# A four-layer cross-attention kernel: layer 2's attention worked in among layer 1's FFN, and layer 3's first queries prepared beside layer 2's gate

## The reference, cut to what matters

```
x = x + tanh(gx[0]) * L0_attn(ctx, ln(x));  x = x + tanh(gf[0]) * L0_ffn(ln(x))
x = x + tanh(gx[1]) * L1_attn(ln(x), ctx);  x = x + tanh(gf[1]) * L1_ffn(ln(x))
x = x + tanh(gx[2]) * L2_attn(ln(x), ctx, ctx);  x = x + tanh(gf[2]) * L2_moe(ln(x))
x = x + tanh(gx[3]) * L3_attn(ln(x), ctx);  x = x + tanh(gf[3]) * L3_ffn(ln(x))

L0_attn: sim = q k'; keep each row's 153 largest; A = sigmoid(sim) * kept; A = (A + A') / 2;
         (1 - gamma) * ln(x) + gamma * A
L0_ffn:  silu(x W1') * (x W3'), Walsh-Hadamard transform over 2048, times W2'
L1_attn: kv = ctx Wk' + bk; s = (ln(x) kv) kv'; softmax(layer_norm(s))
L1_ffn:  "thought" of the last row, four steps of a small MLP; layer_norm(x + sigmoid(x Wg) * thought)
L2_attn: 32 query heads of 16 over 8 key heads of ctx, softmax, values of ctx
```

## Time and profile before

| | |
|---|---|
| median of 3 runs | 4287.12 us (4285.64 to 4291.95) |
| profiled execution | 4288.03 us, its span 4285.8 us |
| PE, DVE, ACT, POOL busy | 3719.1 (87%), 1987.1 (46%), 1372.1 (32%), 362.7 us (8%) |
| mean granted clock of PE | 0.938 of full speed |
| chain that ended last | PE 61%, issue 25%, DVE 7%, ACT 4%, DMA 2% |
| largest transfers of the weights | 4096 KB, two of them 23.9 us to landing |

### The profile page before, as it was taken

One profiled execution on the slowest core, in us unless ns is written; L12 is line 12 of the kernel. 1 busy time (PEld: TensorE's weight loads), 2 busy tenths in 40 slices (PEclk: granted clock), 3 DMA queues, 4 the chain that ended last, 5 costly groups with the idle time before them and its releaser, 6 DMA issues.

```text
span 4285.8 us, 37884 instructions
## 1 busy us (share of the span) xinstructions
PE 3719.1 (87%) x11778; PEld 1714.8 (40%) x11779; DVE 1987.1 (46%) x3526; ACT 1372.1 (32%) x2828; POOL 362.7 (8%) x387
## 2 busy tenths in 40 slices
PE   1899898954658999729987999999999998999999
PEld 0344344421324444316653434434434433444444
DVE  8455554145467777311115665665666663111111
ACT  5424331021125666402223434434434432001000
POOL 6000000000012221031111000000000000000000
PEclk6999999977878999869998999999999999999999
DMA  2321121230031222045554110000000001222221
GB/s 91 135 72 59 59 74 64 69 129 3 0 76 49 54 61 52 32 152 162 163 171 140 43 53 34 23 34 33 23 34 34 22 23 49 78 79 88 76 86 54
DMA packets 77518, 292.43 MB, mean 68 GB/s; under 512 B 10440, under 2 KB 11336, under 8 KB 66252
## 3 DMA queue, kind: packets, MB, share of 16 engines
q1 hardware_dynamic: 69072, 265.17, 19.0%
q0 software_dynamic: 8320, 25.71, 2.0%
HBM read 256.73 MB, written 33.59 MB: 68 GB/s over the span
## 4 chain that ended last, share of the span: by engine, by line
PE 61%; issue 25%; DVE 7%; ACT 4%; DMA 2%; POOL 1%; SPq 1%; POOLq 0%; DVEq 0%; ACTq 0%
PE BM L1824 5%; PE BM L344 5%; PE BR L344 5%; PE BM L1875 5%; PE BR L1883 4%; PE BS L1859 3%; PE BT L1153 3%; PE BS L361 3%; PE BT L361 3%; PE BM L1834 2%; PE BR L1510 2%; PE BM L1499 2%; PE BR L1499 2%; PE BT L1868 2%; PE BM L1848 2%
## 5 line engine op out<-in xcount | busy, mean ns | idle before, releaser
L344 PE MATMUL BM<-XT,AR 128*128 (+1 forms) x1024 | 462.3, 594 | 7.1 <-DMA AR<-l_w_dram 4.9
L344 PE MATMUL BR<-XT,AR 128*128 (+1 forms) x1024 | 460.3, 592 | 0.0
L1935 ACT COPY AR<-BM 128x512 f32<-128x512 f32 x340 | 199.5, 587 | 396.5 <-PE BM L1875 185.8
L1941 ACT ACTIVATE AR<-BS,AR 128x512 f32<-128x512 f32 x256 | 175.7, 690 | 411.5 <-DVE AR L2035 411.5
L344 PEld LDWEIGHTS BM<-XT,AR 128*128 128x128 f32 x1024 | 194.8, 191 | 254.2 <-issue 254.2
L344 PEld LDWEIGHTS BR<-XT,AR 128*128 128x128 f32 x1024 | 194.6, 190 | 244.9 <-issue 244.9
L2048 DVE SCALAR_TENSOR_TENSOR X<-BR,AR,X 128x512 f32<-128x512 f32 x256 | 191.9, 750 | 214.0 <-PE BR L1883 204.8
L399 DVE TENSOR_TENSOR AR<-AR,BR 128x512 f32<-128x512 f32 x80 | 55.0, 687 | 473.6 <-PE BR L344 473.6
L2035 DVE TENSOR_REDUCE AR<-BS 128x2 f32<-128x1024 f32 x128 | 156.9, 1226 | 252.5 <-PE BS L1859 252.5
L1883 PE MATMUL BR<-AR 128*128 128x512 f32 x512 | 255.5, 622 | 3.9 <-DVE X L2048 0.3
L1824 PE MATMUL BM<-XT,AR 128*128 128x512 f32 x512 | 236.5, 605 | 1.3 <-ACT XT L240 1.3
(11 more groups left out here) (326 smaller groups left out, 5349.8 us busy)
## 6 DMA issues: line engine op xcount, KB each, us to landing
AR<-l_w_dram SPq DMA_DIRECT2D x128, 512.0 KB, 3.7
AR<-l_wq_dram SPq DMA_DIRECT2D x32, 1152.0 KB, 5.1
AR<-l_w_dram SPq DMA_DIRECT2D x42, 768.0 KB, 4.9
AR<-w2h SPq DMA_DIRECT2D x16, 1024.0 KB, 4.8
QS<-qx SPq DMA_DIRECT2D x32, 512.0 KB, 9.7
AR<-l_w_dram SPq DMA_DIRECT2D x16, 1024.0 KB, 4.8
AR<-l_w_dram SPq DMA_DIRECT2D x8, 1408.0 KB, 17.5
made<-AR SPq DMA_DIRECT2D x40, 256.0 KB, 5.0
```

The lines of the kernel that those rows point to most:

```text
L344: last = nc.tensor.matmul(bank.rearrange("p (a n) -> p a n", a=1), w[:, kt, a, :], XT[:, ds(b & 1, 1), kt, :], start=kt == 0, stop=kt == K ...
L1935: nc.scalar.copy(to, BM[:, L3[job] % 2, :]).then_inc(m_free, 1)
```

## The change

- Layer 1: the loops over batches are written out on all engines. The projections of batch b + 1 stand before the first unit of batch b and its similarities behind it. The search's 32 steps stand behind units, at most three to a unit and none in the last group, except three before the pairs of group 1. The transposed graph goes into the four S_BANKS (BS and BT) in the last group, behind its first unit. Batch b + 1's norm is made behind the third unit of that group and transposed before the down products.
- Layer 2's attention of batch b - 1 is made inside batch b's FFN: its norm at the start of group 0 (transposed behind the group's units, evicted to XT1), keys in group 1 before the down products and context between the two pairs, scores in group 2, the rest in group 3. Batch 3's is made after the loop. Its operations are those of before (the scores and the context use BM, the keys BM and BR); CTB, POOL's copy of a batch's context, is gone.
- SP: the first up weights are loaded at the very beginning; the weights of layer 2 are loaded inside layer 1's FFN. BC and GATE follow later, GATE into AGG's place. XL's first three rows and the constants are loaded before X's last batch is complete.
- POOL: the root of batch 0's norm stands before `keys_pool`.
- Gate batches: written out. In the second, batch 0's norm for layer 3 is made too, its banks are split straight into QHL, and POOL clears KS2 and QS2. The last batch makes no norm. SP starts layer 3's loads after the first gate batch (x_done 3 * B + 1), and the values (CN2) after the last.

The diff, cut to its core (eight leading spaces left off):

```diff
-STEPS = ((2, 2, 2, 1, 1, 1), (2, 2, 2, 1, 1, 1), (2, 2, 1, 1, 1, 1), (2, 2, 1, 1, 0, 0))
-FOUND_STEP, FOUND_LAST = 5, 7 + ST
+STEPS = ((0, 3, 3, 3, 0, 0), (3, 3, 3, 2, 2, 1), (3, 3, 3, 0, 0, 0), (0, 0, 0, 0, 0, 0))
...
+    sp.wait_ge(l0f.m.free, 2 + ST + HAD_M + 2)
+    sp.dma_start(w2h.rearrange("g p n -> p g n"), WH[1].rearrange("p (g u) n -> p g (u n)", u=UG)).then_inc(wh_stored, 16)
+    sp.wait_ge(wh_stored, 16)
+    down(0)
+    for n in range(1, B * ST):
+        b, g = divmod(n - 1, ST)
+        for u in range(UG):
+            sp.wait_ge(f.r.full, L0["r", b, g, u] + 1)
+            up(n, u)
+        sp.wait_ge(f.s.full, L0["s", b, g] + ST)
+        down(n)
+        if n == 3:
+            sp.wait_ge(kx_stored, 32)
+            sp.dma_start(WK1, l1_wk).then_inc(l1_w, 16)
+            sp.dma_start(BK1, l1_bk).then_inc(l1_w, 16)
+            sp.dma_start(BKR, l1_bk_row.to_broadcast([P, C])).then_inc(l1_w, 16)
+            sp.dma_start(ROWS1, l1_ln.rearrange("(o a) n -> o a n", o=1).to_broadcast([P, 2, S])).then_inc(l1_w, 16)
+        if n == 6:
+            for dst, src in ((AGG, l1_agg), (D1, l1_d1), (COLS, l1_cols)):
+                sp.dma_start(dst, src).then_inc(l1f_w, 16)
+            sp.dma_start(OROWS, l1_rows.rearrange("(o a) n -> o a n", o=1).to_broadcast([P, 2, D])).then_inc(l1f_w, 16)
+        if n == 13:
+            sp.wait_ge(f.s.free, L0["s", 2, ST - 1] + 2 * ST)
+            sp.dma_start(D2, l1_d2).then_inc(l1f_w, 16)
...
+        pe.wait_ge(f.s.free, s.now() + ST)
+        s.step(ST)
         for j in range(ST):
-            bank = start_job(pe, l0f.r, r)
...
+                last = nc.tensor.transpose(S_BANKS[j][:, i * P:(i + 1) * P], GRAPH[:, i, j * P:(j + 1) * P], ID[:, :])
+            last.then_inc(f.s.full, 1)
...
-    with loop(pe, B - 1, (m, L0_M), (r, L0_R), (s, ST * ST), (n_in, ST), (T_PE, KT), (N_PE, 2)) as b:
-        hold(pe, turn.free, T_PE.now() + 2)
-        similarities(b + 1)
-        ffn_tensor_batch(pe, l0f, m, r, s, n_in, b)
-        turn_graph(b + 1)
-        N_PE.step()
-        norm_tensor(pe)
     pe.wait_ge(turn.free, T_PE.now() + 2)
...
+    for b in range(B):
+        for g in range(ST):
+            assert g or b == 0 or L0["s", b, g] == s.now()
+            for u in range(UG):
+                if g == 0 and u == 0 and b < B - 1:
+                    project(b + 1)
+                assert L0["r", b, g, u] == r.now()
+                unit(b, g, u)
+                if g == 0 and u == 0 and b < B - 1:
+                    similarities()
+                if g == ST - 1 and u == 0 and b < B - 1:
+                    turn_graph(b + 1)
+            if g == 0 and b:
+                norm_tensor(pe)
+            if g == 0 and b < B - 1:
+                N_PE.step()
+            if g == 1 and b:
+                l1_keys(b - 1)
+            if g == 2 and b:
+                l1_scores()
+            if g == ST - 1:
+                norm_tensor(pe)
+                if b == B - 1:
+                    l1_keys(b)
+            assert L0["s", b, g] == s.now()
+            down(b, g, 0)
+            if g == 1 and b:
+                l1_context()
+            down(b, g, 1)
+    norm_tensor(pe)
+    l1_context()
+    l1_scores()
...
                 r.step()
-                count(STEPS[g][u])
-            count(STEPS[g][UG] + STEPS[g][UG + 1])
+                if b < B - 1:
+                    if g == 0 and u == 0:
+                        similarities(b + 1)
+                    count(STEPS[g][u])
+            if g == 0 and b:
+                norm_scalar_l1(act)
+            if g == 1 and b:
+                l1_keys()
+                r.step(2)
+            if g == 2 and b:
+                l1_scores(b - 1)
+            if g == ST - 1:
+                norm_scalar(act, (b + 1) & 1)
+                if b == B - 1:
+                    l1_keys()
+                    r.step(2)
+                if b:
+                    l1_exp(b - 1)
+            if b < B - 1:
+                count(STEPS[g][UG])
+            if g == 1 and b:
+                l1_context()
+            if b < B - 1:
+                count(STEPS[g][UG + 1])
         tr.step()
-        r.step(ST)
-        norm_scalar(act, (b + 1) & 1)
-    ffn_scalar_batch(act, l0f, m, r)
-    norm_scalar(act, 0)
+    norm_scalar_l1(act)
+    l1_context()
+    l1_scores(B - 1)
+    l1_exp(B - 1)
...
+    for b in range(B):
+        t = 0
+        if b:
+            norm_turned(b - 1)
+        if b < B - 1:
+            m.step(2)
...
+                    if g == 0 and u == 0:
+                        m.step(ST)
+                        v.wait_ge(f.m.free, m.now() + 2)
+                        begin_search()
+                    search(t, t + STEPS[g][u])
+                    t += STEPS[g][u]
+                if g == ST - 1:
+                    if u == 0 and b:
+                        l1_normed(b - 1)
+                    if u == 1 and b:
+                        l1_max()
+                    if u == 1 and b < B - 1:
+                        add_graph(b + 1)
+                    if u == 2:
+                        norm_turned((b + 1) % B)
+            if g == 0 and b < B - 1:
+                norm_vector(v, b + 1)
+                add_norm(b + 1)
+            if g == 1 and b:
+                l1_keys()
+            if g == 2 and b < B - 1:
+                keep_top()
+                add_top(b + 1)
+            if g == ST - 1 and b == B - 1:
+                l1_keys()
+            for st in range(ST):
+                if st % 2 == 0 and b < B - 1:
+                    search(t, t + STEPS[g][UG + st // 2])
+                    t += STEPS[g][UG + st // 2]
+                if st == 2 and g == 1 and b:
+                    m.step()
+                if st == 2 and g == 2 and b:
+                    l1_moments()
+                if st == 2 and g == ST - 1 and b:
+                    l1_add(b - 1)
...
+    norm_turned(B - 1)
+    m.step()
+    l1_moments()
+    l1_normed(B - 1)
+    l1_max()
+    l1_add(B - 1)
...
+    had_pool(pool)
+    norm_pool(pool)
+    keys_pool(pool)
+    for b in range(B):
+        if b:
+            norm_pool(pool)
+        if b < B - 1:
+            norm_pool(pool)
+        if b:
+            root1(b - 1)
+        norm_pool(pool)
+    norm_pool(pool)
+    root1(B - 1)
...
+    sp.wait_ge(x_done, FFN0_DONE)
...
+    for b in range(B):
+        if b == B - 1:
+            sp.wait_ge(x_done, 3 * B)
+        sp.dma_start(XL[b:b + 1, :], X[P - 1:P, b * ST + ST - 1, :]).then_inc(xl_in, 16)
+    sp.dma_start(BC, l1_bc).then_inc(l1f_late, 16)
+    sp.wait_ge(lr.full, 1)
+    sp.dma_start(GATE, l1_gate).then_inc(l1f_late, 16)
...
+        if b == 1:
+            norm_tensor(pe)
...
+        if b == 1:
+            for kt in range(KT):
+                nc.scalar.copy(QHL[:, 0, kt, :], full(act, turn, T_ACT)).then_inc(q_hi, 1)
...
+        if b == 1:
+            norm_vector(v, 0)
+            for kt in range(KT):
+                bank = turn.banks[:, (T_V.now() + kt) % 2, :]
+                v.wait_ge(q_hi, kt + 1)
+                nc.vector.tensor_tensor(QHL[:, 1, kt, :], bank, QHL[:, 0, kt, :].bitcast(F32), ALU.subtract).then_inc(turn.free, 1)
+            T_V.step(KT)
+            v.wait_ge(turn.free, T_V.now() + 2)
+            v.sem_inc(q_cut, KT)
+        if b < B - 1:
+            norm_vector(v, b + 1)
+            T_V.step(KT)
...
+        if b == 1:
+            norm_pool(pool)
+            pool.wait_ge(norm_rstd, N_P.now())
+            nc.gpsimd.memset(KS2[64:KR, :, :].bitcast(F32), 1.0).then_inc(k_ones, 1)
+            for g in range(KVH):
+                pool.wait_ge(q_zero, g) if g else pool.wait_ge(k_ones, 1)
+                nc.gpsimd.memset(QS2[64:KR, 4 * g:4 * g + 4, :].bitcast(F32), 0.0).then_inc(q_zero, 1)
+            pool.wait_ge(q_zero, KVH)
+        if b < B - 1:
...
+    sp.wait_ge(x_done, 3 * B + 1)
+    def values():
+        sp.wait_ge(x_done, 4 * B)
...
+    values()
...
-    nc.scalar.copy(QHL[:, 0, :, :], XT[:, 0, :, :]).then_inc(q_hi, KT)
...
-    v.wait_ge(q_hi, KT)
-    nc.vector.tensor_tensor(QHL[:, 1, :, :], XT[:, 0, :, :], QHL[:, 0, :, :].bitcast(F32), ALU.subtract).then_inc(q_cut, KT)
-    for g in range(4):
-        nc.vector.memset(QS2[64:KR, 4 * g:4 * g + 4, :].bitcast(F32), 0.0).then_inc(q_zero, 1)
...
-    for g in range(4, KVH):
-        pool.wait_ge(q_zero, g)
-        nc.gpsimd.memset(QS2[64:KR, 4 * g:4 * g + 4, :].bitcast(F32), 0.0).then_inc(q_zero, 1)
```

More of the change, by code:

```diff
@@ new lines, in down @@
+            def down(b, g, pair):
+                if pair == 0:
+                    pe.wait_ge(f.down_in, (b * ST + g + 1) * 16)
+                else:
+                    pe.wait_ge(turn.free, T_PE.now() + 2)
+                pe.wait_ge(f.s.free, s.now() + 2)
+                s.step(2)
+                for u in range(UG):
+                    if pair == 0:
+                        pe.wait_ge(f.r.free, freed[u])
+                    for j in range(2):
+                        st = 2 * pair + j
```

(51 more changed lines are left out.)

381 lines of the change are left out of this document (171 added, 210 removed).

## The result

The changed kernel takes 4150.78 us (median of 4 runs, 4149.39 to 4152.34) where the one before took 4286.65 in the same comparison (4285.64 to 4291.95): ratio 0.9681, 95% interval 0.9664 to 0.9697. The forecast was 4161.0, the range 4142 to 4184. The profiled execution took 4149.84 us with a span of 4148.0, so the spans differ by 137.8; the prediction's terms came to 126.2.

| stretch | before | after | difference | predicted |
|---|---|---|---|---|
| to PE's first projection | 134.43 | 118.80 | -15.6 | -13.0 |
| four FFN batches | 750.2 | 748.9 | -1.3 | -0.2 |
| FFN's end to X's last addition | 137.2 | 40.8 | -96.4 | -96.7 |
| X to the first thought | 7.5 | 1.8 | -5.7 | -4.6 |
| thoughts | 107.7 | 107.3 | -0.4 | 0 |

A forecast was written before the change was run, and what follows sets the result against it. PE was taken to bound layer 1's FFN, with serial chains behind it. Terms -13.0 - 0.2 - 96.7 - 4.6 + 18.2 - 29.9 = -126.2 us take 4288.0 to 4161.8; the median, 0.9 lower, gives 4161.0, range 4142 to 4184.

The forecast's parts named there:

- 1. Start of the FFN: Before layer 1's first FFN projection: four graph banks and POOL's earlier root let XN's transposes start earlier, -13.0 us.
- 2. The FFN: Layer 1's four FFN batches, with three batches of layer 2's attention inside: 750.0 us against 750.2, -0.2 us.
- rival A: FFN group 0: no hole, ACT reaches the turned banks between the counts or counts run early; -14.7 us, 4146, chance 0.12.
- Rival B: FFN units: three search steps do not fit a unit, PE waits for HIDDEN; +27 us at most, 4188, chance 0.14.
- 3. Rest of the attention: Behind layer 1's FFN: only batch 3's attention chain is left, 40.5 us in place of 137.2, -96.7 us.
- Rival E: Attention parts wait for each other inside the FFN and PE stands still; +51 us, 4212, chance 0.04.
- 4. Thoughts: From X to the first thought: one transfer left behind X instead of eleven, -4.6 us.
- 5. Gate batches: Layer 2's gate batches: +20.5 us in the second from POOL's memsets between roots, -2.3 in the last; +18.2, bounds +9.5, +22.
- the upper value: Second gate batch: memsets leave additions alone and meet only the norm's TENSOR_SCALARs; +19.1 us for the stage.
- 6. Layer 3's start: From X to layer 3's first scores: query transfers done before X is complete, scores within 0.3 us of X, -29.9 us.
- rival C: Layer 3's start: the queries' early start does not pay, something else is as late; +29.9 us, 4191, chance 0.04.
- Rival D: Written-out loops of layers 1 and 2: instruction fetch makes the kernel slower than before; 4331 us, chance 0.02.

## Why the prediction was right

**1. Start of the FFN, -15.6 for -13.0.** The mechanism is shown by the kernel with the split first. The size was off in two terms: the Hadamard products end at 115.65 and not 116.8, and the two sets of transposes with their evictions, for which I took the 4.63 of the row before, take 3.15. In that row PE had waited 11.20 us ahead of them, and here it had not: a duration taken from behind a wait that the change removes is too long.

**2. The FFN, -1.3 for -0.2.** By batches: 177.3, 195.0, 196.5 and 180.2 us where I had 177.6, 196.25 twice and 179.9. The hole was 5.59 us long, priced with 0.24 of it as the normal hand-over: 5.35. Behind the two holes the lower clock cost 1.45 and 2.9 us, where I had 2 each. It is shown by its removal that ACT's order makes the hole, so rival A is out. Rival B is out by the 0.60 us that DVE waits at three steps; the run with four loses 12 us, but where the keys want BR, and not at each unit as B has it. What paid for three batches of attention are the stretches between the batches: PE had waited 34.8 us in them for X and XN (three times some 4.2 and 7.4), and these waits are gone.

**3. Rest of the attention, -96.4 for -96.7.** The kernel with all four chains behind the FFN shows both sides: 119.5 us outside against 51.4 inside. Rival E, which had the attention cost the FFN another 51 us in standing still, is out.

**4. Thoughts, -5.7 for -4.6.** The transfer's landing and issue cost 1.8 in place of 2.9. No run isolates it.

**5. Gate batches, +13.3 for +18.2.** The second batch was right in size (+20.3 for +20.5): POOL's 19 us between the roots set it, as the run that frees DVE's XN and gains nothing shows, and moving the memsets out gives 8.3 back. But the sign that I had named for it, DVE waiting 4 to 8 us for the second root, did not come; it waited 1.20. Of two engines' hindrance I expected POOL to lose up to 1.9 us. It lost 0.67 (15.47 for eight memsets, 14.80 in the run where XN comes first), and DVE lost 8.0, which the sum did not have. DVE was ready for the second root 0.05 us behind POOL. That the time does not show this loss is luck: what DVE had lost beyond it would have lengthened the stage. Which instructions meet is seen in the rows: the TENSOR_SCALARs of XN took 9.89 us beside the memsets, and in the run with the early clearing the SCALAR_TENSOR_TENSOR of the mix, which reads GT and XT from SBUF, took 0.75 us beside the memset of KS2, the same as in the changed kernel without one. This agrees with the Trainium skill, SBUF — State Buffer, section "Who interferes with whom", by which memsets meet the TENSOR_SCALARs and leave alone additions that read two SBUF operands; the upper value that I worked out beside it put the loss on the wrong engine. What the step lacked in its sum is that the loop was written out: it carried over 3.6 us of hand-overs that belong to the register loop. The last batch gave 3.4 where I had 2.3.

**6. Layer 3's start, -29.8 for -29.9.** The run with the late transfer brings 27.5 back, so rival C is out. Rival D, the cost of written-out code, is out too: PE's units take 6.87 us here as before, and in the gate stage the written-out form is the faster one.

Behind the first scores nothing was predicted, and -1.8 us lie within the 3003 to 3011 us that this stretch took in all runs. Together the eight differences make 137.7 of the 137.8 us.

The prediction held because the change moves whole chains whose length stood in the trace, into holes that did too. Its two largest errors, 2.6 and 4.9 us, had one sign, and the larger part of each (1.5 and 3.6 us) is a duration taken over from a place with a wait or a loop that the change also removes.

The one theory that fell is that of the four steps. It looked at one ring of two banks and the units that use it, and forgot that another user, the keys, takes both banks right behind them.

## What to carry to other kernels

- Put a serial chain beside a busy engine piece by piece, and ask at each piece which queue its evictions stand in. Here three badly placed steps of the search, in each of two batches, cost some 14 us, a quarter of what all the inserted work cost, and moving them by one place gave this back.
- Clearing and constants are no free filler for an idle engine if the same engine owes a small result (a root) to the critical path in between: spread them, and put each part into a gap that holds it. In the first gate batch POOL had 17.5 us between two roots; 14.7 us of memsets put there cost nothing.
- Slack counted against one producer's buffers holds only until the next user of the same buffers; look who takes both of a pair.

## What the runs showed of the hardware

- A row of four 128x512 TENSOR_SCALARs on DVE, 1.91 us alone, took 9.89 us while POOL cleared 64-partition tiles, and POOL's eight memsets took 15.47 in place of 14.80. The loss is nearly all DVE's. In the trace it looks like slow instructions, not like a wait: DVE's tile XN has a median of 543 ns, and here one instruction took 3812 ns, beside a memset of 3.51 us, and the other three some 2104 each, beside memsets of 1.9 us. A SCALAR_TENSOR_TENSOR with two SBUF operands kept its 0.75 us beside a memset.
- A hole on PE costs more than its length, and not always the same. Two holes of 5.35 us cost 6.8 and 8.3, and behind a wait of 3.92 us sixteen products of 7.03 us took 9.48. The granted clock was 0.50 (1.2 GHz) right behind the first hole, from 338 to 340 us, and 0.55 behind the second, from 533 to 540. Behind a wait of 1.79 us the same products lost nothing in one trace and 1.2 us in another.
- The end of a register loop costs DVE 0.62 us of idle time in every round of the gate stage, and a wait on a register's value 0.16 us ahead of each addition, where the waits on constants had none.
